# Last stage of a two-layer decoder: four PSUM banks for VectorE and two for ScalarE instead of three each

## The reference, cut to what matters

```
h = bit_linear(x, w1)                    # x quantised per token, w1 ternary: 512 -> 2048
h = depthwise_conv1d(h, conv_w, conv_b)  # three taps along the tokens
h = silu(h)
y = bit_linear(h, w2)                    # h quantised per token, w2 ternary: 2048 -> 512
x = layernorm(x + y)
```

## Time and profile before

| | |
|---|---|
| timed runs | 2627.15 us median of 3 (2626.56 to 2629.21) |
| profiled execution | 2629.23 us, of which 2627.4 us span |
| PE busy | 2365.7 us (90%) |
| DVE busy | 1579.9 us (60%) |
| ACT busy | 1245.8 us (47%) |
| POOL busy | 687.0 us (26%) |
| mean granted TensorE clock | 0.977 of full |
| stage f, first to last f_g, batches 0, 1, 2 | 563.6 to 677.2, 1205.3 to 1319.0, 1847.1 to 1960.8 |
| the same, batch 3 | 2488.8 to 2593.0 |

### The profile page before, as it was taken

One profiled execution on the slowest core, in us unless ns is written; L12 is line 12 of the kernel. 1 busy time (PEld: TensorE's weight loads), 2 busy tenths in 40 slices (PEclk: granted clock), 3 DMA queues, 4 the chain that ended last, 5 costly groups with the idle time before them and its releaser, 6 DMA issues.

```text
span 2627.4 us, 37008 instructions
## 1 busy us (share of the span) xinstructions
PE 2365.7 (90%) x12984; PEld 1311.6 (50%) x13000; DVE 1579.9 (60%) x3101; ACT 1245.8 (47%) x2870; POOL 687.0 (26%) x989
## 2 busy tenths in 40 slices
PE   7889999988988999998898999988889899999867
PEld 3655544445465544444556554444455655444344
DVE  4664633468866462447877655165787746516688
ACT  5753312258675422127868341222886823122396
POOL 0002221026401232013720213101480021310266
PEclk9999999999999999999999999999999999999888
DMA  8001101010210200001030110001003010100000
GB/s 298 18 10 50 46 20 33 0 49 1 85 52 10 71 29 17 32 1 49 9 127 2 47 34 29 32 17 43 7 9 127 2 57 23 45 1 1 0 1 33
DMA packets 58987, 99.41 MB, mean 38 GB/s; under 512 B 13364, under 2 KB 13748, under 8 KB 58296
## 3 DMA queue, kind: packets, MB, share of 16 engines
q1 hardware_dynamic: 58808, 97.06, 11.2%
HBM read 88.66 MB, written 8.39 MB: 37 GB/s over the span
## 4 chain that ended last, share of the span: by engine, by line
PE 63%; DVE 16%; ACT 15%; issue 4%; POOL 0%; DMA 0%; ACTq 0%; DVEq 0%; POOLq 0%; SPq 0%
PE psum L396 22%; PE psum L390 17%; ACT prob L801 6%; PE psum L474 3%; DVE neg_max L1095 3%; PE psum L540 2%; DVE f_a L1102 2%; PE psum L782 2%; ACT xT L829 1%; PE psum L754 1%; DVE f_top L1382 1%; DVE f_g L1372 1%; PE psum L560 1%; ACT f_z L997 1%; PE psum L611 1%
## 5 line engine op out<-in xcount | busy, mean ns | idle before, releaser
L390 PE MATMUL psum<-xT,weights 128*128 128x512 f32 x1152 | 508.9, 595 | 16.6 <-DMA weights<-in_a_k 10.3
L390 PEld LDWEIGHTS psum<-xT,weights 128*128 128x128 f32 x1152 | 214.9, 191 | 265.7 <-issue 246.6
L396 PE MATMUL psum<-weights,mixed 128*128 128x512 f32 x768 | 338.8, 597 | 0.0
L801 ACT ACTIVATE prob<-psum,neg_max 128x128 f32<-128x128 f32 (+3 forms) x512 | 264.9, 543 | 109.6 <-DVE neg_max L1095 109.6
L396 PE MATMUL psum<-weights,xT 128*128 128x512 f32 x640 | 289.0, 596 | 2.4 <-DVE recip L1285 1.6
L1420 POOL TENSOR_SCALAR var<-stats 128x1 f32<-128x1 f32 x192 | 61.1, 318 | 792.5 <-DVE stats L1046 792.5
L1095 DVE TENSOR_REDUCE neg_max<-psum 128x1 f32<-128x128 f32 (+3 forms) x512 | 217.0, 481 | 81.3 <-PE psum L479 46.6
L1433 POOL TENSOR_TENSOR f_a<-f_a,f_z 128x256 f32<-128x256 f32 x256 | 199.6, 788 | 133.6 <-DVE f_a L1102 127.0
L396 PEld LDWEIGHTS psum<-weights,mixed 128*128 128x128 f32 x768 | 144.4, 191 | 179.8 <-issue 179.0
L1076 DVE TENSOR_TENSOR x<-psum,x 128x512 f32<-128x512 f32 x128 | 88.3, 690 | 225.3 <-PE psum L396 163.2
L829 ACT COPY xT<-psum 128x512 f32<-128x512 f32 x128 | 67.1, 596 | 327.7 <-PE psum L427 327.7
(11 more groups left out here) (242 smaller groups left out, 4034.1 us busy)
## 6 DMA issues: line engine op xcount, KB each, us to landing
xT<-in_xT SPq DMA_DIRECT2D x8, 1024.0 KB, 6.3
x<-in_x SPq DMA_DIRECT2D x8, 1024.0 KB, 8.8
out<-x SPq DMA_DIRECT2D x16, 512.0 KB, 2.8
weights<-in_a_k SPq DMA_DIRECT2D x4, 1024.0 KB, 5.4
weights<-in_a_q SPq DMA_DIRECT2D x4, 1024.0 KB, 5.1
weights<-in_a_v SPq DMA_DIRECT2D x4, 1024.0 KB, 5.0
w1f<-in_w SPq DMA_DIRECT2D x4, 1024.0 KB, 14.8
w2f<-in_w SPq DMA_DIRECT2D x4, 1024.0 KB, 17.3
```

The costliest lines, as they stand in the source:

```text
L390: last = mm(bank[:, 0:n], weights[weight][:, c, heads(g)], rhs(c), start=(c == 0), stop=(c == C - 1))
L396: last = mm(bank, lhsT(c), weights[weight][:, c, :], start=(c == 0), stop=(stop and c == C - 1))
L801: last = run(sb["prob"][:, slot, o:o + keys], bank[:, o:o + keys], ACT.Exp, bias=sb["neg_max"][:, n, qc, j:j + 1], accum_out=sb["a_sum"][: ...
```

## The change

At the first hidden tile of each batch TensorE waits until both rings are drained, and from there `act_ring` has banks 0 and 1 and `dve_ring` banks 2, 3, 4 and 5. At the end of the next batch's stage a they are set back to 0 to 2 and 3 to 5. Nothing else is changed: no instruction of any engine but the waits and bank numbers.

```diff
@@ class Ring
+    def move(self, pe, banks):
+
+        self.drained(pe)
+        self.banks = banks
@@ TensorE
                 elif kind == "a_end":
                     for ring in (a_ring, turn_ring, turn_act_ring):
                         ring.drained(pe)
+                    act_ring.banks, dve_ring.banks = banks[0:3], banks[3:6]
@@ TensorE, f_hidden
                     if m == 0 and s < W:
                         taken(pe, ("f_unit", s))
                         pe.wait_ge(q["f_pad"], at("f_pad", 4))
+                    if s + m == 0:
+                        act_ring.move(pe, banks[0:2])
+                        dve_ring.move(pe, banks[2:6])
                     bank = dve_ring.claim(pe, step)
```

## The result

| | before | after |
|---|---|---|
| timed, median (range, runs) | 2627.57 us (2626.53 to 2629.21, 6) | 2641.32 us (2639.43 to 2643.4, 6) |
| ratio, with its 95% interval | | 1.0052 (1.0041 to 1.0063) |
| profiled execution, its span | 2629.23, 2627.4 us | 2641.35, 2639.5 us |
| mean granted clock | 0.977 | 0.976 |
| tile 0 to the next batch's first a_score, batches 0, 1, 2 | 141.58, 141.57, 141.59 us | 144.45, 146.74, 146.77 us |

What follows compares the result with a forecast made beforehand. In batch 0's stage f the bound moves between ScalarE, VectorE and TensorE; in batch 3 VectorE leads. Three batches at +1.8 us plus +0.5 in batch 3 give +5.9, 2633.0 us (own range 2628 to 2638; 8 in 10: 2624 to 2642).

Steps and rivals of the forecast that it cites:

- early shift of VectorE (tile 15): First f_g behind the n = 14 projection, batches 0 to 2: +3.85 us from ScalarE's two banks, +2.0 from the clock.
- won back up to n = 43: Projections at n = 21, 28, 35, 42: VectorE's fourth bank returns 1.48, 0.55, 0.75 and 0.67 us, 3.45 in all.
- from there to the last tile: After n = 43 VectorE leads and has little to win: 0.3 us earlier.
- the stage's end: Batches 0 to 2: ScalarE's 0.51 us wait for f_scale goes, no more can be gained; -0.5 us (0 to -0.5).
- The drain: At tile 0 TensorE waits for both rings to be empty: 0 us, at most 2.5 us over 4 times.
- Two banks for ScalarE: a_key 1 waits for a_value 0's copy and starts 5.0 us later: ScalarE's f_unit copy +3.15 us, VectorE +3.85 us.
- The clock at a_key 1: Batches 0 to 2: behind TensorE's gap a_key 1 begins at 1.2 GHz; +2.0 us (0 to 3.44).
- Four banks for VectorE: TensorE's lead grows by one claim, cutting VectorE's waits behind projections: -3.8 us a batch (1.5 to 7.2 gained).
- Batch 3: No a_key; f_unit's matmul +1.4 us, carried by VectorE, with some given back: +0.5 us (0 to +1.4).
- Little is won back: Early loss stands, a_key 1 wholly at 1.2 GHz, only first projection pays: +5.3 us a batch, 2643.5 us; chance 0.14.
- The clock stays up: One f_turn breaks the gap before a_key 1, so no clock loss: -0.2 us a batch, 2627 us; chance 0.18.

Runs made afterwards that it cites:

- five-and-one kernel: Against the kernel before: from tile 20 of each batch VectorE's ring has five banks and ScalarE's one; 2641.21 us, ratio 1.0045.
- late move: Against the kernel before: four banks for VectorE and two for ScalarE only from tile 20, VectorE's ring not drained; 2619.36 us, ratio 0.9974.
- two and three: Against the kernel before: ScalarE's ring gets two banks from tile 0, VectorE's keeps three, one bank idle; 2651.52 us, ratio 1.0093.

## Why the prediction was right in sign and short in size

| term, us a batch | forecast | batch 0 | batch 1 |
|---|---|---|---|
| early shift of VectorE (tile 15) | +3.85 +2.0 = +5.85 | +5.91 | +6.48 |
| won back up to n = 43 | -3.45 | -2.70 | -2.69 |
| from there to the last tile | -0.3 | +0.11 | +0.13 |
| the stage's end | -0.5 | -0.45 | +1.24 |
| stage | +1.55, taken as +1.8 | +2.87 | +5.16 |

- **The drain**: 0 forecast, 0 measured in a run of its own.
- **Two banks for ScalarE.** Right to the step. a_key 1 moves by 4.99 us (5.0), ScalarE's idle time is 4.51 = 2.45 + the 2.06 of the slow projection (2.4 before the clock), f_unit's matmul is 6.39 later (4.3 + 2.0), and VectorE's part without the clock is 3.84 in the run with a busy TensorE (3.85).
- **The clock at a_key 1.** 2.06 us in batch 0 and 2.6 in batches 1 and 2, for 2.0; right for the first and 0.6 short for the others. The low level lasted some 4.1 us of the projection in batch 0 (582.22 to 586.3) and 5.3 in batch 1 (1229.6 to 1234.9), where 3.3 had been taken from batch 3; that 2.0 fits batch 0 is in part luck, since the sum at 3.3 was 1.65. The fall came in each of the three batches, which agrees with the Trainium skill, "TensorE: Matmul & The Clock Gate", section "HAM oscillation — how this bites in real kernels", on waits that recur. It also came in all three batches at the stall that the five-and-one kernel makes in another place.
- **Four banks for VectorE.** n = 21 won 1.42 (1.48), n = 28 0.52 (0.55), n = 42 0.60 (0.67). From n = 28 to n = 35 the shift falls by 0.16 where 0.75 was forecast. The wait behind n = 35 did shrink by 0.70 (1.99 to 1.29), but what n = 28 had won was already lost: the shift is +3.96 at tile 29 and +4.51 at tile 30, as it was at tile 28. Between the two VectorE never waits, and one tap is longer, stretched beside a GpSimd product. First after, then before:

```profile
620.85 1.27 POOL L383 TENSOR_TENSOR f_y<-f_y,f_s2b 128x512 f32<-128x512 f32 x1
621.25 1.15 DVE L1111 SCALAR_TENSOR_TENSOR f_a<-f_g,conv_w,f_a 128x256 f32<-128x256 f32 x1
```

```profile
619.02 1.27 POOL L378 TENSOR_TENSOR f_y<-f_y,f_s2b 128x512 f32<-128x512 f32 x1
...
619.98 0.60 DVE L1102 SCALAR_TENSOR_TENSOR f_a<-f_g,conv_w,f_a 128x256 f32<-128x256 f32 x1
```

  Before, VectorE's longer wait let most of GpSimd's operation pass first (0.31 us of overlap, a tap of 0.60); with the wait shortened the two overlap for 0.87 us, and the 0.55 us just won go into the tap. That GpSimd's product stretches it was read and not tested; the loss of 0.55 us at this tile stands in every kernel that has four banks there, also in those whose earlier shift differs. The prediction kept VectorE's durations. After n = 43 nothing came back, where 0.3 was forecast.
- **The stage's end: the step that failed.** It said that a wait of 0.5 us goes and nothing more can happen. In batch 0 it did (-0.45). In batches 1 and 2 it is +1.24 and +1.25: the fall of the clock that the kernel before has in front of the last f_scale comes behind it, on the matmuls for which VectorE waits. TensorE's 2.56 us of catching up in front of f_scale are 1.2 from shorter waits, as in the run with TensorE kept busy before a_key 1, and the rest from doing that work at the full clock; the wait of 2.06 us behind it is the other side of this. The run with TensorE busy behind f_scale takes the fall away, and with it 1.7 and 1.8 us. The prediction asked who gains from the shorter wait and did not look for the fall that already stood there, nor for where it would come to lie. Its price for the clock was that of one fall a batch; here a second one had a price. In all the clock cost 2.05 + 4.33 + 4.34 = 10.7 us of stage length (the difference to the run with TensorE busy before a_key 1), of the 12.1 us by which the profiled execution grew, where 6.0 had been forecast.
- **Batch 3.** f_unit's matmul moved by 1.44 us (+1.4), but it was not carried: VectorE's f_g is +2.18 late at tile 10, +0.11 at tile 11 and -0.85 at the last. Before, that matmul stood at the low clock and took 2.04 us, and VectorE waited 2.07 us behind it; after, it takes 1.14. Between tiles 43 and 50 another 0.74 us are won in this batch, as in the late move (0.76) and not in the kernel with two and three. The forecast of +0.5 had the wrong sign; measured -1.07.

The sum of the misses, against the profiled execution: about 3.5 us for the end in two batches (1.75 each), 3.0 for what was not won back (1.0 in each of three, against the +1.8 taken), 1.3 for the slower a_key 1, less 1.6 in batch 3, is 6.2: the 12.1 less the 5.9.

Two rivals had a part of the truth. "Little is won back" came nearest by its number (2643.5) and not by its mechanism: 2.6 us a batch were won back. "The clock stays up" came near what the banks alone do: +0.83 us a batch in the run where a_key 1 runs at the full clock, for the -0.2 given.

**Open.** Why the clock falls in front of the last f_scale in most batches, behind it in batches 1 and 2 of the changed kernel, and not at all in five batches with the same wait of 2.06 us. The rows show no difference in the work right in front. So the size of the second term could not have been forecast from them, though its place could have been looked at.

## What to carry to other kernels

A bank given to one reader's ring is taken from another's; look for the loser's most crowded claims and for what its reader does between two of them, and move the bank only after that. Here the same four and two banks cost 13.75 us from tile 0 and bring 7.7 from tile 20 and 6.9 from tile 14, by the stage lengths. And where the granted clock falls somewhere in a stage, ask which engine waits for the work behind the fall, before and after the change: in front of the last f_scale it was free in every kernel with a fourth bank, behind it it cost 1.7 us.

## What was not expected of the hardware

- A single wait of 4.84 us on one instruction cost TensorE another 2.06 to 2.65 us at 1.2 GHz, about half of its own length, and 40 unread matmuls of 4.56 us in it took all of that away.
- Equal waits of 2.06 us behind the last f_scale came in two batches with a granted clock of 0.50 behind them, and 5.31 us for 16 matmuls, and in five batches with 1.00 and 3.63.
- With a fourth bank the same fall of the clock costs 1.7 us or nothing, by where it lies: 3 us behind the start of the last f_scale, or some 6 us in front of it.
- A VectorE tap of 0.60 us took 1.15 us beside a GpSimd product. The Trainium skill, "Advanced Engine Details and Errata", section "DVE Details", says that one of VectorE's two ports is shared with GpSimd; the two taps shown above agree with it in that the longer overlap (0.87 us for 0.31) has the longer tap.
